# Seven of the eight slices of the second chunk's mixing, issued inside the first down output instead of as a block ahead of it

## The chip, the core and the metric

The kernel runs on one core of one Trainium2 chip. The metric is the device time of one execution in microseconds (us), lower is better; three executions were taken, and the median counts. A core has TensorE (PE, with its weight loads as PEld), VectorE (DVE), ScalarE (ACT), GpSimd (POOL) and SyncE (SP), which run their own instruction streams in order and wait for each other through semaphores.

## The reference, cut to what matters

```python
# x (64, 64, 1024), cond (64, 128); K = 8 experts
h   = gelu(cond @ W0 + b0); h = gelu(h @ W1 + b1)
att = softmax(h @ W2 + b2)
agg_w = einsum('bk,koi->boi', att, weight[..., 0])     # a 64 x 64 mixing matrix per batch
agg_b = att @ bias_k
y   = einsum('boi,bih->boh', agg_w, x) + agg_b[:, :, None]
# three ternary linear layers, w -> round(clip(w / (mean|w| + eps), -1, 1)) * mean|w|
out = x + bitlinear(bitlinear(y, w_gate) * bitlinear(y, w_up), w_down)   # 1024 -> 2752 -> 1024
```

## The kernel before

The 4096 rows of x are worked off in 8 chunks of 512 tokens. Per chunk there are three stages on TensorE. The **mixing** (`conv(c, k)`, L698) multiplies x by the block-diagonal matrices of the mixing in KH = 8 slices of 128 columns of H, each slice as four f32 products, which the trace shows as eight records. Slice k goes to one of two PSUM banks, `YB[k % 2]`; from slice 2 on it waits until VectorE has taken slice k - 2 out (`s_yv`, L710). Slice 1 of chunk 1 also waits for the scales of chunk 0 (`s_p2v`) and for transposed tiles that used its bank (L708). Then come the **gate and up** products and last the **down** products.

Chunk 0 is worked in the plain way while the weights come in: 21 full tiles of gate and of up, each followed by transposes of the next quantised weight tiles, in an order that is written out by hand (`order0`, L119 to L153). The last up tile and the last transposes are the last entries of it. ScalarE copies each transposed tile out of PSUM (`copy_T`, L1072; the copies of a tile of w_down are L1092, L1095 and L1098) and counts it on `s_te`, NQ in all. Chunks 1 to 7 use a seven-product scheme in pairs (`product`, L829) and grouped down products (`down_group`, L899); chunk c + 1 is mixed inside these, one slice per pair. Chunk 1 has no such place, so it is mixed as a block between the up tiles and the down outputs of chunk 0 (L977). This is where the change is.

`down(c, d)` (L806) makes one of DN = 8 outputs of 128 tokens x 512 columns of chunk 0: one matmul with the leftover rows (`inter_r`) and two for each of FT = 21 tiles f, 43 in all, in bank `DNB[d % 2]`. Output 0 waits for all weight tiles (`s_te` at NQ, L812) and, tile by tile, for VectorE's low halves (`s_ulo`, L817 and L822). Output d waits for VectorE to have added output d - 2 to xr (`s_o`, L810). `downs` (L943) issues the eight outputs and, when there is a next chunk, behind output 0 the matmul `norms(c + 1)`, which waits for the sum l1 of all eight slices of y (L723), and behind output 1 `norms_T(c + 1)`, four one-column matmuls that wait for p2b (L728), which VectorE makes in `scales`.

On VectorE the order is by hand as well: slice 0 of chunk 1's mixing is taken out (`conv`, L1349, ys at L1360), then the last `split` of chunk 0 (L1571, L1488), then slices 1 to 7. Behind slice k comes the sum of the magnitudes of slice k - 1 (L1375), for which ScalarE makes |y| (`magnitudes`, L1011). Then (L1599 to L1636):

```python
            for j in range(EARLY, first):
                combine(j)
            output(0, 0)
            scales(1)
            for k in range(KH):
                scale_y(1, k)
            sum_quarter(1, S1)
            lo_quarter(1, A11)
            output(0, 1)
```

and so on through output 7, with ten more combinations of weight blocks between the outputs. `combine(17)` to `combine(20)` (L1500; first tensor_tensor at L1509 or L1506) make the weight sums of the seven-product scheme in two staging buffers; ScalarE fills part of them (`copies`), GpSimd stores them to DRAM (L648), and a buffer is used again when its store has landed. `scales(c)` (L1377) reads the norms matmul and writes p2b at L1389. SyncE stores output d when `s_o` has counted it, loads the first ring blocks of the combined weights behind output 5 (L584 to L588), and the first combined down weights behind the last output (L593).

Of the kernel before, what the change touches and what calls it, by code (L numbers as in the profile page):

```python
# [5 lines left out]
def adaln_ternary_ffn(nc: bass.Bass, x, cond, w0, b0, w1, b1, w2, b2, wk, bias_k, w_gate, w_up, w_down, out):  # L6
# [18 lines left out]
    KH = H // P  # L25
# [49 lines left out]
    def hidden(n):  # L75

        return n if n < NG else (n - 1) % NG

    summed = [e for e, (n, s, _, _) in enumerate(loads) if s]
    q_load = {n: e for e, (n, _, q, _) in enumerate(loads) if q}  # L80
    assert len(summed) == NQ and sorted(q_load) == list(range(NQ))

# [74 lines left out]
    with ctx:  # L157
# [64 lines left out]
        def raw(e):  # L222
            n, _, _, s = loads[e]
            return slot(*s)[0:tiles[n][1], 0:tiles[n][2]]

        def part(f, i):

            return inter[:, f, :].bitcast(f16)[:, i * TOK:(i + 1) * TOK]
# [426 lines left out]
        def _(pe):  # L655
            def mm(o, l, r, start=True, stop=True):
                return nc.tensor.matmul(o, l, r, start=start, stop=stop)  # L657
# [40 lines left out]
            def conv(c, k):  # L698

                if k == 0:  # L700
                    pe.wait_ge(s_x, 16 * (c + 1))
                    pe.wait_ge(s_ablk, 2 * (c + 1))
                if k == 0 and isinstance(c, int) and c == 0:
                    pe.wait_ge(s_bbv, 1)
                if k == 1 and not (isinstance(c, int) and c == 0):
                    pe.wait_ge(s_p2v, c)
                    if isinstance(c, int) and c == 1:
                        pe.wait_ge(s_te, max(n for n in range(NQ) if n % 3 == 2) + 1)  # L708
                if k >= 2:
                    pe.wait_ge(s_yv, KH * c + k - 1)  # L710
                for t in range(NT):
                    last = mm(YB[k % 2][:, t * P:(t + 1) * P], xa[:, t, k * P:(k + 1) * P], ablk[:, t, :])
                last.then_inc(s_y, 1)
# [56 lines left out]
            def waited(c):  # L770

                if not isinstance(c, int):
                    pe.sem_inc(s_turn_pe, 1)

            def group(c, j):

                if j < 4:
                    if isinstance(c, int) and c == 0:
                        if j:
                            pe.wait_ge(s_agg1, j)  # L780
                    else:
                        pe.wait_ge(s_uv, UP * c)
                elif j - 4 < FT:
                    pe.wait_ge(s_gv, FT * c + j - 3)
                else:
                    pe.wait_ge(s_uv, UP * c + j - 3 - FT)
                waited(c)
                for n, k in enumerate(FIRST_K if j == 0 else range(KH)):
                    if j == 0:
                        pe.wait_ge(s_ylo, KH * c + n + 1)  # L790
                        waited(c)
                    if j < FT:
                        w = wgT[:, k, j * P:(j + 1) * P]
                    elif j == FT:
                        w = wrT[:, k, :]
                    else:
                        w = wuT[:, k, (j - UP) * P:(j - UP + 1) * P]
                    if isinstance(c, int) and c == 0 and j == 0 and n == KH // 2:
                        pe.wait_ge(s_te, 1)
                    if isinstance(c, int) and c == 0 and j == 0 and n == 6:  # L800
                        transpose(1)
                    for i in range(2):
                        last = mm(GUB[j % 4][:, :], w, yp[:, k, i, :], start=(n + i == 0), stop=(n == KH - 1 and i == 1))
                last.then_inc(s_gu, 1)

            def down(c, d):  # L806

                t, n = d // HB, d % HB
                if d >= 2:
                    pe.wait_ge(s_o, DN * c + d - 1)  # L810
                elif isinstance(c, int) and c == 0:
                    pe.wait_ge(s_te, NQ)  # L812
                else:
                    pe.wait_ge(s_o, DN * c)
                cols = slice(n * TOK, (n + 1) * TOK)
                if d == 0:
                    pe.wait_ge(s_ulo, UP * c + 1)  # L817
                waited(c)
                mm(DNB[d % 2][:, :], inter_r[:, t * P:(t + 1) * P], wdT[:, FT, cols], start=True, stop=False)
                for f in range(FT):  # L820
                    if d == 0:
                        pe.wait_ge(s_ulo, UP * c + f + 2)  # L822
                        waited(c)
                    for i in range(2):
                        last = mm(DNB[d % 2][:, :], part(f, i)[:, t * P:(t + 1) * P], wdT[:, f, cols],
                                  start=False, stop=(f == FT - 1 and i == 1))
                last.then_inc(s_dn, 1)
# [115 lines left out]
            def downs(c, more):  # L943
                for d in range(DN):
                    down(c, d)
                    if more and d == 0:
                        norms(c + 1)
                    if more and d == 1:
                        norms_T(c + 1)
# [16 lines left out]
            for what, n in order0:  # L966
# [7 lines left out]
                elif what == "U":  # L974
                    pe.wait_ge(s_te, NG + n + 1)
                    group(0, FT + n)
            for k in range(KH):  # L977
                conv(1, k)
            downs(0, True)

            def pairs(c, more):
# [864 lines left out]
```

## Time and profile before

| | us |
|---|---|
| median of 3 executions (lowest, highest) | 1734.46 (1733.05, 1734.97) |
| the profiled execution | 1734.24 |
| its span, first to last instruction | 1732.4 |
| TensorE busy | 1705.4 (98%) |
| VectorE busy | 1097.0 (63%) |
| ScalarE busy | 576.4 (33%) |
| mean granted TensorE clock (1 is 2.4 GHz) | 0.996 |

The profile is of one execution. Times in the trace are counted from the first instruction of the span. An engine's busy time is what the sum of its instructions covers; matmuls are pipelined, so that the recorded length of a matmul (0.38 us for 512 columns) is longer than the distance to the next one. In a timeline, neighbouring instructions of the same kind are merged into one row.

### The profile page before, as it was taken

What the parts mean: (1) busy time and instruction counts of PE and PEld (TensorE: products, weight loads), DVE (VectorE), ACT (ScalarE), POOL (GpSimd) and SP (SyncE); (2) the same over time, 40 slices, a digit from 0 to 9 for tenths busy, and PEclk for the clock granted to TensorE, in tenths of its full rate; (3) what the DMA queues carried; (4) which work ended last, traced back from release to release, by engine and by line L of the source; (5) the groups of instructions that cost most, each with busy time, mean ns of one, the idle gap of its engine ahead of it and who ended that gap; (6) DMA issues with size and microseconds to landing.
All of it is one profiled execution on the core that took longest, in us unless ns stands there. A gap on an engine that the chain in (4) does not pass through costs nothing.

```text
span 1732.4 us, 31273 instructions
## 1 busy us (share of the span) xinstructions
PE 1705.4 (98%) x12380; PEld 1209.9 (70%) x12388; DVE 1097.0 (63%) x1785; ACT 576.4 (33%) x921; POOL 29.2 (2%) x57
## 2 busy tenths in 40 slices
PE   5999999999999999999999999999999999999999
PEld 3454555977769596795958868597776958678584
DVE  5888896555765458554685546855576555855464
ACT  6777742312333133231333213231233313333120
POOL 0010001000000000000000000000000000000000
PEclk8999999999999999999999999999999999999999
DMA  9656725412232121410224121331223312132021
GB/s 341 248 199 236 252 93 190 148 46 97 75 123 101 41 107 65 180 65 22 107 95 170 65 75 54 121 142 45 97 75 111 112 43 107 65 123 74 31 90 49
DMA packets 59687, 194.06 MB, mean 112 GB/s; under 512 B 5264, under 2 KB 5712, under 8 KB 59536
## 3 DMA queue, kind: packets, MB, share of 16 engines
q1 hardware_dynamic: 56464, 177.62, 28.9%
q0 software_dynamic: 2480, 14.22, 2.2%
q8 instruction: 109, 1.79, 0.4%
q14 instruction: 42, 0.34, 0.1%
q10 hardware_dynamic: 592, 0.09, 0.0%
HBM read 160.90 MB, written 31.01 MB: 111 GB/s over the span
## 4 chain that ended last, share of the span: by engine, by line
PE 96%; SPq 1%; DMA 1%; DVE 1%; ACT 1%; issue 0%; DVEq 0%
PE ps L877 52%; PE ps L934 24%; PE ps L657 16%; PE ps L895 2%; SPq L526 1%; DMA wuT<-in_L_ffn_w_gate_dram 1%; PE ps L757 1%; ACT aT L261 0%; DVE msk L1438 0%; DVE xa L1509 0%; DVE prod L1476 0%; ACT wdT L1092 0%; SPq L490 0%; DVE xa L1512 0%; ACT wgT L1108 0%
## 5 line engine op out<-in xcount | busy, mean ns | idle before, releaser
L877 PE MATMUL ps<-yp,wgT 128*128 128x256 f16 x4116 | 902.6, 273 | 2.4 <-issue 2.2
L877 PE MATMUL ps<-wuT,wgT 128*128 128x256 f16 x4116 | 902.6, 273 | 0.0
L877 PEld LDWEIGHTS ps<-yp,wgT 128*128 128x128 fp8e4 x4116 | 402.9, 98 | 53.1 <-issue 5.3
L877 PEld LDWEIGHTS ps<-wuT,wgT 128*128 128x128 fp8e4 x4116 | 402.7, 98 | 48.3
L934 PE MATMUL ps<-wdT,inter 128*128 128x512 fp8e4 x1960 | 433.2, 379 | 0.0
L934 PEld LDWEIGHTS ps<-wdT,inter 128*128 128x128 f16 x1960 | 191.2, 98 | 227.0 <-issue 1.4
L1743 DVE SCALAR_TENSOR_TENSOR xr<-ps,osc,xr 128x512 f32<-128x512 f32 x210 | 156.6, 749 | 168.0 <-PE ps L934 128.4
L1692 DVE TENSOR_TENSOR wdT<-ps,msk 128x512 f32<-128x512 f32 (+1 forms) x77 | 51.3, 667 | 207.1 <-PE ps L877 207.1
L1221 ACT COPY raw<-ps 128x512 f32<-128x512 f32 (+1 forms) x77 | 43.6, 567 | 316.5 <-PE ps L877 315.9
L1228 ACT COPY msk<-ps 128x512 f32<-128x512 f32 (+1 forms) x77 | 43.6, 567 | 140.5 <-PE ps L877 140.5
L1243 ACT COPY inter<-ps 128x256 f32<-128x256 f32 x70 | 26.1, 372 | 180.1 <-PE ps L877 180.1
L1726 DVE TENSOR_TENSOR inter<-inter 128x1024 f16<-128x1024 f32 x70 | 85.3, 1219 | 0.0
L1185 ACT CAST yp<-ys 128x1024 f16<-128x1024 f32 x49 | 48.5, 1042 | 101.8 <-DVE ys L1393 59.0
L1656 DVE TENSOR_TENSOR wdT<-ps,raw 128x512 f32<-128x512 f32 x70 | 48.4, 692 | 44.8 <-PE ps L877 44.3
L657 PE MATMUL ps<-yp,wgT 128*128 128x512 f16 x336 | 76.1, 379 | 0.1
L657 PE MATMUL ps<-yp,wuT 128*128 128x512 f16 x336 | 75.1, 379 | 0.0
L657 PE MATMUL ps<-wdT,inter 128*128 128x512 fp8e4 x336 | 73.8, 379 | 0.0
L1251 ACT CAST inter<-inter 128x1024 f16<-128x1024 f32 x70 | 73.3, 1047 | 0.0
L1247 ACT CAST inter<-prod 128x768 f16<-128x768 f32 x35 | 29.1, 832 | 132.7 <-DVE prod L1696 132.7
L1678 DVE TENSOR_TENSOR wdT<-ps,raw 128x512 f32<-128x512 f32 (+1 forms) x77 | 50.9, 661 | 33.2 <-ACT raw L1235 33.2
L1247 ACT CAST inter<-wuT 128x768 f16<-128x768 f32 x35 | 29.1, 832 | 127.7 <-DVE wuT L1696 127.7
L657 PE MATMUL ps<-ablk,xa 128*128 128x128 f32 x512 | 69.8, 283 | 1.1 <-DMA xa<-in_x_dram 0.7
(224 smaller groups left out, 1488.6 us busy)
## 6 DMA issues: line engine op xcount, KB each, us to landing
wgT<-wcomb SPq DMA_DIRECT2D x70, 896.0 KB, 4.7
wdT<-dcomb SPq DMA_DIRECT2D x14, 2240.0 KB, 10.4
xa<-in_x_dram SPq DMA_DIRECT2D x8, 2048.0 KB, 7.9
out_dram<-xr SPq DMA_DIRECT2D x64, 256.0 KB, 2.0
wcomb<-xa POOLq DMA_DIRECT2D x17, 448.0 KB, 3.6
xr<-in_L_ffn_w_down_dram SPq DMA_DIRECT2D x9, 512.0 KB, 5.6
inter<-in_L_ffn_w_gate_dram SPq DMA_DIRECT2D x7, 512.0 KB, 16.1
wdT<-in_L_ffn_w_up_dram SPq DMA_DIRECT2D x7, 512.0 KB, 4.2
```

What stands on the lines that cost most here:

```text
L657: return nc.tensor.matmul(o, l, r, start=start, stop=stop)
L877: last = nc.tensor.matmul(out, w, operand(i, OPERAND[what])[:, k, :], start=(start and h + k + i == 0), stop=(k == KQ - 1 and i == 1), ski ...
L934: last = nc.tensor.matmul(bank[:, :], x, wd_block(p, BLOCK[what]), start=(what in ("P1", "P2", "P5") and q + i == 0), stop=(q == GRP - 1 a ...
L1185: nc.scalar.copy(operand(0, s), quarter(s)).then_inc(s_yhi, 1)
L1221: nc.scalar.copy(t1[:, 0:w], PB[p % 2][:, 0:w]).then_inc(s_t1, 1)
L1247: nc.scalar.copy(pair_parts(p, 0, 0, 3), blocks4[p % 2][:, HALF:4 * HALF]).then_inc(s_hiA, 1)
L1251: nc.scalar.copy(pair_parts(p, 0, 3, 4), sums).then_inc(s_hiS, 1)
L1656: V.tensor_tensor(rr if p < NPR else g21, PA[:, 0:w], t1[:, 0:w], ALU.add).then_inc(s_c11, 1)
L1678: V.tensor_tensor(rr[:, TOK - w:TOK], PC[p % 2][:, 0:w], q67[:, 0:w], ALU.add).then_inc(s_c22, 1)
L1692: V.tensor_tensor(rr[:, 0:w], PC[p % 2][:, 0:w], q6[p % 2][:, 0:w], ALU.add).then_inc(s_c12, 1)
L1726: V.tensor_tensor(pair_parts(p, 1, 3, 4), sums, pair_parts(p, 0, 3, 4), ALU.subtract).then_inc(s_loS, 1)
L1743: V.scalar_tensor_tensor(xr[:, t, cols], bank[:, :], osc[:, t:t + 1], xr[:, t, cols], ALU.mult, ALU.add).then_inc(s_o, 1)
```

## The change

In `down`, behind the wait for tile f of output 0, slice f // 3 + 1 of the mixing of chunk 1 is issued if f is a multiple of 3 (f = 0, 3, ..., 18 give slices 1 to 7). The block ahead of the down outputs keeps slice 0 alone. `down` is used for chunk 0 only. Only TensorE's stream is changed; the streams of the other engines are as they were.

```diff
@@ -821,6 +821,8 @@
                     if d == 0:
                         pe.wait_ge(s_ulo, UP * c + f + 2)
                         waited(c)
+                        if f % 3 == 0 and f // 3 in range(KH):
+                            conv(1, f // 3 + 1)
                     for i in range(2):
                         last = mm(DNB[d % 2][:, :], part(f, i)[:, t * P:(t + 1) * P], wdT[:, f, cols],
                                   start=False, stop=(f == FT - 1 and i == 1))
@@ -974,8 +976,7 @@
                 elif what == "U":
                     pe.wait_ge(s_te, NG + n + 1)
                     group(0, FT + n)
-            for k in range(KH):
-                conv(1, k)
+            conv(1, 0)
             downs(0, True)
 
             def pairs(c, more):
```

## Rows read from the trace of the kernel before

**Rows 1.** The page: TensorE's busy time, and the chain that ended last.
```profile
PE 1705.4 (98%) x12380; PEld 1209.9 (70%) x12388; DVE 1097.0 (63%) x1785; ACT 576.4 (33%) x921; POOL 29.2 (2%) x57
...
PE 96%; SPq 1%; DMA 1%; DVE 1%; ACT 1%; issue 0%; DVEq 0%
```

**Rows 2.** Timeline of TensorE: start, length, instruction, count, idle time before and releaser.
```profile
214.07 4.30 PE L657 MATMUL ps<-ablk,xa 128*128 128x128 f32 x32
218.59 4.04 PE L657 MATMUL ps<-ablk,xa 128*128 128x128 f32 x32 [0.22 <-DVE ys L1360]
222.46 0.38 PE L657 MATMUL ps<-wdT,inter_r 128*128 128x512 fp8e4 x1
222.68 9.23 PE L657 MATMUL ps<-wdT,inter 128*128 128x512 fp8e4 x42
231.96 0.38 PE L657 MATMUL ps<-wdT,inter_r 128*128 128x512 fp8e4 x1
...
241.34 0.25 PE L657 MATMUL ps<-onesb,l 1*128 1x1 bf16 x4
241.52 0.39 PE L657 MATMUL ps<-wdT,inter_r 128*128 128x512 fp8e4 x1
```

**Rows 3.** Timeline of TensorE in chunk 0's mixing: one slice, then the next matmul.
```profile
21.03 1.05 PE L657 MATMUL ps<-ablk,xa 128*128 128x128 f32 x8
21.92 0.38 PE L718 MATMUL ps<-ab,onesb 128*128 128x512 bf16 x1
```

**Rows 4.** Timeline of ScalarE: the last copies of the last transposed tile.
```profile
216.42 0.55 ACT L1098 ACTIVATE wdT<-ps 64x128 fp8e4<-64x128 fp8e4 x2
```

**Rows 5.** Timeline of VectorE beside the mixing and the down outputs.
```profile
215.88 0.68 DVE L1488 TENSOR_TENSOR inter<-prod,inter 128x512 f16<-128x512 f32 x1
...
222.67 0.68 DVE L1360 TENSOR_TENSOR ys<-ps,bbc 128x512 f32<-128x512 f32 x1
...
224.05 0.42 DVE L1375 TENSOR_TENSOR l<-l,ab 128x512 bf16<-128x512 bf16 x1 [0.36 <-ACT ab L1022]
224.40 1.22 DVE L1509 TENSOR_TENSOR msk<-wuT 128x1024 fp8e4<-128x1024 fp8e4 x1
...
230.20 1.23 DVE L1509 TENSOR_TENSOR msk<-wuT 128x1024 fp8e4<-128x1024 fp8e4 x1 [0.55 <-DMA wcomb<-msk]
...
235.48 0.75 DVE L1497 SCALAR_TENSOR_TENSOR xr<-ps,osc,xr 128x512 f32<-128x512 f32 x1
...
237.66 0.41 DVE L1389 CAST l<-p 1x512 bf16<-1x512 f32 x1
...
245.19 0.74 DVE L1497 SCALAR_TENSOR_TENSOR xr<-ps,osc,xr 128x512 f32<-128x512 f32 x1
...
278.85 0.75 DVE L1497 SCALAR_TENSOR_TENSOR xr<-ps,osc,xr 128x512 f32<-128x512 f32 x1 [1.90 <-PE ps L657]
...
288.13 0.75 DVE L1497 SCALAR_TENSOR_TENSOR xr<-ps,osc,xr 128x512 f32<-128x512 f32 x1 [2.22 <-PE ps L657]
```

**Rows 6.** Timeline of TensorE: the two longest stops behind the start.
```profile
36.21 4.49 PE L657 MATMUL ps<-inter 128*64 128x448 f32 x12 [6.68 <-ACT msk L1051]
43.35 0.38 PE L657 MATMUL ps<-tot,ones 128*128 128x1 f32 x2 [2.66 <-DVE tot L1417]
```

**Rows 7.** Windows: stretch, its length, TensorE busy (instructions), granted clock, DMA share, GB/s.
```profile
29.00:30.00 1.00, 0.25 (x4) 1.00 1.02 406
30.00:31.00 1.00, 0.00 (x0) 0.53 1.02 406
40.00:41.00 1.00, 0.69 (x4) 0.85 0.96 197
43.00:44.00 1.00, 0.65 (x3) 0.86 0.10 41
47.00:48.00 1.00, 1.00 (x4) 0.93 0.80 328
```

## The prediction

> **What bounds the kernel now.** I read the page first. TensorE is busy 98% of the span and holds 96% of the chain that ended last [rows 1]: whatever makes TensorE stand still, anywhere, is paid in full, unless it stood still there already. Then the timeline of TensorE over the changed stretch [rows 2]. The reader is to see two blocks there. The mixing of chunk 1 (64 records, eight slices of eight) runs from 214.07 to 222.46, 8.39 us, with one recorded idle time of 0.22. Behind it the down outputs follow each other without a gap: the first from 222.46, the second from 231.96, the third from 241.52. From 222.46 to 231.96 there are 44 matmuls (1 + 42 and the norms matmul), so one costs 0.216 us and an output of 43 costs 9.28.
>
> Is the mixing block at TensorE's own pace? Where a slice stands between other matmuls, the next instruction follows its start by 0.89 us (21.03 to 21.92) [rows 3]. Eight such slices are 7.1 us, so the block holds 1.3 us of waiting: slice k needs the bank of slice k-2, and VectorE takes about 1.0 us per slice (0.68 for ys, 0.42 for l1). That waiting is all that spreading the slices can win on TensorE.
>
> Last I read who is busy beside it. ScalarE still copies the last transposed w_down tile until 216.42 + 0.55 = 216.97 [rows 4], which is under the mixing block. VectorE [rows 5] does the last slice at 222.67, its l1 at 224.05, and then from 224.40, nearly without a gap, the four combinations 17 to 20, output 0 at 235.48, the scales with p2b at 237.66, eight scalings, and so on; it first waits for TensorE at 278.85. TensorE waits for none of this today: p2b is there at 238.07 and is wanted at 241.34, output 0 is there at 236.2 and is wanted at 241.52. The covers are 3.3 and 5.3 us.
>
> **The change part by part.** No instruction is added or dropped; seven slices (56 of the 64 records) move behind f = 0, 3, ..., 18 of output 0. No DMA is moved on any queue, and SyncE and GpSimd keep their order.
>
> (a) Removed: the waiting inside the block. Between two slices now lie six matmuls, 1.3 us, so slice plus matmuls (2.2 us) is longer than VectorE's 1.1. Gain 1.3 us.
>
> (b) The down output needs all tiles (s_te at NQ). Slice 0 ends at about 214.07 + 0.93 = 215.0; the last copy lands at 216.97. Today slices 1 to 7 hide that. Now TensorE waits until about 217.05: 2.0 us lost. Behind this wait on TensorE stand slices 1 to 7 too, and so all of VectorE's work behind them. The wait for s_ulo at f = 20 costs nothing: the last split is done on VectorE right behind slice 0, at 215.88, nine microseconds and more before it is asked for. Nor does the bank of slice 1, whose transposes are long done.
>
> (c) The last slice now ends late. From 217.05: 37 matmuls x 0.216 = 8.0 and 7 slices x 0.89 = 6.2, which is 231.3 against 222.46. VectorE is in order: combinations 17 to 20 stand behind its slice 7. Today ys starts 0.21 behind the end of the slice on TensorE and the first combination 1.73 behind that [rows 5]; so it starts at about 233.2 instead of 224.40, 8.8 us later. VectorE's idle time between the slices is lost.
>
> (d) The norms matmul stands behind output 0 and needs l1 of slice 7. TensorE gets there after six more matmuls, at 232.6; l1 is done at about 233.3: 0.7 us lost. Then 0.22 and 9.28 for output 1: TensorE is at norms_T at 242.8.
>
> (e) norms_T needs p2b. Everything between 224.40 and 238.07 on VectorE is its own work but for 0.55 us on a staging store, which moves along with it (its store is issued by GpSimd behind combination 17). So p2b is there at 238.07 + 8.8 = 246.9: TensorE waits **4.1 us**. Output 2, which also needs output 0 from VectorE (236.2 + 8.8 = 245.0), is covered by that wait.
>
> (f) After that: output 3 needs output 1's accumulation, 245.19 + 0.74 + 8.8 = 254.7, and TensorE wants it at 247.1 + 9.28 = 256.4. It fits by 1.7 us; the later ones fit by more, since their covers were larger. VectorE's delay shrinks by its waits of 1.90 at 278.85 and 2.22 at 288.13 to TensorE's own delay of 5.6. Nothing is late when the products begin. The stores of the combinations and the loads behind them had waits that are longer than the delay, or are released by the down outputs.
>
> Sum: 2.0 + 0.7 + 4.1 - 1.3 = 5.5; directly, norms_T moves from 241.34 to 246.9, 5.6. From there on everything on TensorE lies 5.6 later. The profiled execution took 1734.24 us against a median of 1734.46 and a span of 1732.4, so the sum is made against 1734.24: **1739.8**. Ends of the terms: a slice between f16 matmuls costs 0.89 to 0.97 (its 1/8 of the best stretch in the block, 218.59 to 222.46), up to 0.6 us in all; the semaphore steps 0.2 each way; the staging wait between 0 and 1.1. So 5.0 to 6.6.
>
> (g) The clock. A wait of 4.1 us is not in the sum only by its length. In the trace TensorE stood still for 6.68 us before 36.21 and for 2.66 before 43.35 [rows 6]. The granted clock [rows 7] went to 0.5 (1.2 GHz instead of 2.4) at about 30.0, was back at about 40.3, fell again in the slice 43 to 44 (mean 0.86, so at about 43.7) and rose in 47 to 48 (at about 47.1). So both long stops were followed by the lower level; TensorE then worked 4.1 us and 3.4 us at it, half of which is lost: 2.0 and 1.7 us. Below, the price is nothing, if the clock stays. No row has a stop of 4.1 us, but it lies between these two, and I take the nearer one's 1.7. The stop of 2.0 us in (b) is shorter than either; I count nothing for it, and up to 1.7 in the range.
>
> Of this the Trainium skill speaks in "TensorE: Matmul & The Clock Gate", the section "Why this matters for your kernels": it warns against idle gaps between bursts of matmuls, since such a gap brings TensorE back to the half rate. By that rule the change, which opens a gap in a stretch that has none, costs the 5.6 us and the slow start behind it; without the rule only the 5.6. The trace agrees with it at the two stops above.
>
> Forecast: 1734.24 + 5.6 + 1.7 = **1741.5**.
>
> **The rivals.**
> 1. The same waits, but the clock stays at 2.4 GHz: 1739.8. For it: the last stop before the fall at 30.0 came after sparse work, while here TensorE is dense on both sides. Against: both stops of over 2.5 us fell.
> 2. Both new stops (2.0 and 4.1 us) lower the clock: the first makes slice 7 and so p2b up to 1.7 us later, the second costs 1.7 to 2.0: 1743.3 or so. Against: no stop as short as 2.0 us is seen with a fall.
> 3. VectorE is less late than I count, and p2b is not what TensorE waits for; then (a), (b) and (d) are left: 2.0 + 0.7 - 1.3 = +1.4, 1735.6. It decides if VectorE's chain from 224.40 to 238.07 could be shortened by over 4 us. Against: it shows 0.55 us of idle time.
> 4. The other side: not slower. The place is L1360, for which the block waits; spreading removes 1.3 us, and if the copies of the last tile came before 215.0 and VectorE's work had room, 1734.24 - 1.3 = 1732.9 would stand, a difference under what can be told. The turning points are 216.97 against 215.0, and 3.3 us of cover for p2b against 8.8 of delay. The rows speak against both.
> 5. The change does not do what it says: if the slices were issued as before, nothing would move. The code leaves no room for that: f // 3 runs over 0 to 6, so slices 1 to 7 are all issued in output 0, once each. I give it no chance.
>
> **How the numbers follow.** Forecast 0.50, rival 1 0.26, rival 2 0.14, rival 3 0.07, rival 4 0.03. A measurement of this kernel tells about 0.2% from no change, 3.5 us: between 1731.0 and 1737.9 is "same". The forecast and rivals 1 and 2 are slower by more: 0.89 with a little taken off for a sum that is short by 2 us. Rivals 3 and 4 are within it: 0.10. Faster by over 0.2%: 0.01, since at most 1.3 us can be won. The range: rival 1 with the lower end of the terms is 1734.2 + 5.0 = 1739.2, less 0.7 for the spread of the runs: 1738.5. Rival 2 with the upper ends, 1734.2 + 6.6 + 1.7 + 1.7 = 1744.2: 1744.0. Left out are rivals 3 and 4 and the tails, some 0.15.
>
> **What would show it.** In the trace of the changed kernel: TensorE idle about 2.0 us behind slice 0, released by the ScalarE copy of L1098; about 0.7 before the norms matmul; about 4.1 before the four one-column matmuls of norms_T, released by L1389 on VectorE, at about 247; combination 17 at about 233 instead of 224.40; a granted clock under 1 for three to four microseconds behind 247. The outputs 2 to 7 then without a gap, and the first product some 5.6 to 7.3 us later than today. It is wrong if VectorE starts combination 17 well before 232, if norms_T follows output 1 without a wait, or if a second large wait appears in outputs 3 to 7 (then VectorE, not p2b alone, has become the bound, and the time is above the range).

## The result, and the profile after

The changed kernel takes 1743.9 us (median of 4, 1742.66 to 1745.44) against 1734.01 us (median of 4) for the kernel before; the ratio is 1.0055, with a 95% interval of 1.0042 to 1.0067. It is slower by 9.9 us in the medians. The profiled execution took 1742.93 us with a span of 1741.1, 8.7 more than the span before.

The timeline of TensorE in the changed kernel (start, length, instruction, count, idle time before and its releaser) answers to [rows 2]:

```profile
213.96 1.16 PE L657 MATMUL ps<-ablk,xa 128*128 128x128 f32 x8
216.90 0.39 PE L657 MATMUL ps<-wdT,inter_r 128*128 128x512 fp8e4 x1 [1.79 <-ACT wdT L1099]
217.13 1.05 PE L657 MATMUL ps<-ablk,xa 128*128 128x128 f32 x8
218.02 1.46 PE L657 MATMUL ps<-wdT,inter 128*128 128x512 fp8e4 x6
...
230.24 1.05 PE L657 MATMUL ps<-ablk,xa 128*128 128x128 f32 x8
231.13 1.46 PE L657 MATMUL ps<-wdT,inter 128*128 128x512 fp8e4 x6
233.43 0.38 PE L657 MATMUL ps<-wdT,inter_r 128*128 128x512 fp8e4 x1 [0.84 <-DVE l L1376]
233.65 9.23 PE L657 MATMUL ps<-wdT,inter 128*128 128x512 fp8e4 x42
246.78 0.26 PE L657 MATMUL ps<-onesb,l 1*128 1x1 bf16 x4 [3.90 <-DVE l L1390]
246.97 0.61 PE L657 MATMUL ps<-wdT,inter_r 128*128 128x512 fp8e4 x1
247.37 11.65 PE L657 MATMUL ps<-wdT,inter 128*128 128x512 fp8e4 x42
258.86 0.38 PE L657 MATMUL ps<-wdT,inter_r 128*128 128x512 fp8e4 x1
```

Three stops are new: 1.79 us for the last transposed tile, 0.84 ahead of the norms matmul for l1, 3.90 ahead of norms_T for p2b. Between two slices there is no stop any more: a slice (0.89) and six matmuls (1.29) follow each other every 2.18 us. The three stops are 6.53 us, while norms_T moves from 27.27 to 32.82 us behind slice 0 (241.34 - 214.07 and 246.78 - 213.96), so about 1.0 us of waiting inside the block was won. And output 2 takes 11.89 us (246.97 to 258.86) where output 1 takes 9.3.

VectorE's timeline, which answers to [rows 5], shows why p2b is late. It idles 1.2 us before nearly every slice, then does after 233.06 what it did before the change after 224.40:

```profile
229.15 0.69 DVE L1361 TENSOR_TENSOR ys<-ps,bbc 128x512 f32<-128x512 f32 x1 [1.16 <-PE ps L657]
...
231.33 0.69 DVE L1361 TENSOR_TENSOR ys<-ps,bbc 128x512 f32<-128x512 f32 x1 [1.16 <-PE ps L657]
...
233.06 1.22 DVE L1510 TENSOR_TENSOR msk<-wuT 128x1024 fp8e4<-128x1024 fp8e4 x1
...
238.87 1.23 DVE L1510 TENSOR_TENSOR msk<-wuT 128x1024 fp8e4<-128x1024 fp8e4 x1 [0.55 <-DMA wcomb<-msk]
...
246.31 0.41 DVE L1390 CAST l<-p 1x512 bf16<-1x512 f32 x1
```

The windows of TensorE behind the long stop (stretch, its length, busy, granted clock, DMA share, GB/s) show the other part:

```profile
244.00:246.00 2.00, 0.00 (x0) 0.86 0.26 101
246.00:248.00 2.00, 1.22 (x7) 0.50 0.69 264
248.00:250.00 2.00, 2.00 (x7) 0.50 0.00 0
250.00:252.00 2.00, 2.00 (x6) 0.50 0.00 0
252.00:254.00 2.00, 2.00 (x10) 0.93 0.00 0
```

The clock falls at about 245.4, inside the stop (the first window's mean is 0.86), and is back at about 252.3. That is 6.8 us at the lower level; 1.3 of them lie inside the stop, and TensorE works the other 5.5 us at 1.2 GHz.

To keep the parts apart, each kernel below is read in three stretches of its profile: to the start of slice 0 of chunk 1; from there to the first product of chunk 1 (**the down stretch**, where the change is); and from that product to the end of the span (**the loop stretch**). The first is not touched by the edits down to run 8, and still varies between their profiles (213.5 to 215.9 us). Before the change the others are 297.21 - 214.07 = 83.14 and 1732.4 - 297.21 = 1435.19. In the changed kernel the first product is at 305.26, so they are 91.30 and 1435.84: +8.16 and +0.65.

### The profile page after: what moved, and what is told of

Read it like the earlier page. It is cut to its first block, busy times and chain, and to the rows that moved or that the text cites. A ratio compares the mean times of both kernels' runs of the same rounds, so it can differ in the third digit from the quotient of the medians.

```text
span 1741.1 us, 31279 instructions
## 1 busy us (share of the span) xinstructions
PE 1707.2 (98%) x12380; PEld 1210.3 (70%) x12388; DVE 1096.8 (63%) x1785; ACT 576.6 (33%) x921; POOL 29.5 (2%) x57
## 3 DMA queue, kind: packets, MB, share of 16 engines
q8 instruction: 109, 1.79, 0.4%
## 4 chain that ended last, share of the span: by engine, by line
PE 95%; SPq 1%; DMA 1%; DVE 1%; issue 1%; ACT 0%; DVEq 0%; ACTq 0%; POOLq 0%
PE ps L879 52%; PE ps L936 24%; PE ps L657 16%; PE ps L897 2%; SPq L526 1%; DMA wuT<-in_L_ffn_w_gate_dram 1%; PE ps L757 1%; DMA wcomb<-msk 0%; DVE msk L1439 0%; DVE xa L1510 0%; DVE prod L1477 0%; ACT wdT L1093 0%; SPq L490 0%; DVE xa L1513 0%; DVE msk L1510 0%
```

## The experiments

All medians stand beside those of the kernel before on the same chip: 1734.72 us for the first four kernels, 1734.28 for the next four, 1733.96 for the three with early matmuls, 1733.49 for the last. Runs 1 to 5 start from the changed kernel, runs 7 and 9 to 11 from the kernel before.

**1. Filling the long stop.** To hold the clock without touching the wait:

```diff
                     if more and d == 1:
+                        for _ in range(16):
+                            mm(ps[0][:, :], part(0, 0)[:, 0:P], wdT[:, 0, 0:TOK])
                         norms_T(c + 1)
```

> The changed kernel with 16 more matmuls of 512 columns between output 1 and norms_T; their result (bank 0) is not used. They take 16 x 0.216 = 3.5 us out of the 3.9 us in which TensorE waits for p2b, so TensorE is idle for 0.4 us and never stops. Theory (the wait costs its length, 5.6 us in all, and on top the lower clock behind it, 2.6 us in the profiled run): norms_T at the same place, about 246.8; the granted clock stays at 1; output 2 takes 9.3 us and not 11.9; 1734.0 + 5.6 = 1739.6 against 1743.9. Rival (output 2 is slow because VectorE or a transfer disturbs it, or the extra comes from elsewhere): 1743 to 1744, output 2 still about 11.9.

Measured: 1750.42 us, ratio 1.0084 (1.0069 to 1.01). That is neither of the two. The trace has to be read by stretches. TensorE around norms_T:

```profile
235.12 12.68 PE L657 MATMUL ps<-wdT,inter 128*128 128x512 fp8e4 x58
248.27 0.25 PE L657 MATMUL ps<-onesb,l 1*128 1x1 bf16 x4 [0.47 <-DVE l L1392]
248.45 0.39 PE L657 MATMUL ps<-wdT,inter_r 128*128 128x512 fp8e4 x1
...
257.74 0.38 PE L657 MATMUL ps<-wdT,inter_r 128*128 128x512 fp8e4 x1
```

Slice 0 starts at 215.43 here, so norms_T comes 32.84 us behind it, as in the changed kernel (246.78 - 213.96 = 32.82): the wait is where it was, TensorE only does something in it. The clock stays at 1, and output 2 takes 9.29 us instead of 11.89. The down stretch is 88.71, 5.57 over the kernel before. So the theory holds where the change is: 5.6 us for the waits, 2.6 for the clock. But the loop stretch, which the edit does not touch, is 1444.86, 9.7 us longer. Runs 9 to 11 take that up.

**2. The slices closer together.** At f = 0 to 6 instead of 0, 3, ..., 18:

```diff
-                        if f % 3 == 0 and f // 3 in range(KH):
-                            conv(1, f // 3 + 1)
+                        if f + 1 in range(1, KH):
+                            conv(1, f + 1)
```

> The changed kernel with slices 1 to 7 at f = 0 to 6 instead of f = 0, 3, ..., 18: the same number of slices in output 0, only closer. Theory (how late the last slice is decides, because VectorE's work stands behind it): last slice ends at 217.05 + 0.2 + 6 x 1.33 + 0.9 = 226.1, 3.7 later than before the change, p2b at 241.8; TensorE is there at 241.3 + 2.0 - 1.3 = 242.0. No wait at norms_T, no fall of the clock; what is left is 2.0 for the last transposed tile less 1.3 of waiting in the block: 1734.0 + 0.7 = 1734.7. Rival (interleaving as such costs, by switches between the two kinds of matmul or by VectorE and TensorE disturbing each other): 1738 or more.

Measured: 1736.26 us, 1.0009 (1.0 to 1.0018). The down stretch is 83.94, 0.80 over the kernel before. norms_T follows without a stop; of the new stops only the one for the last tile is left:

```profile
218.82 0.39 PE L657 MATMUL ps<-wdT,inter_r 128*128 128x512 fp8e4 x1 [1.78 <-ACT wdT L1099]
...
243.94 0.25 PE L657 MATMUL ps<-onesb,l 1*128 1x1 bf16 x4
244.12 0.39 PE L657 MATMUL ps<-wdT,inter_r 128*128 128x512 fp8e4 x1
```

Interleaving as such shows no cost here; spreading the slices over the whole output has one. The median is 1.5 us over that of the kernel before; in the profile, 0.8 us is in the down stretch and 0.9 in the loop stretch (1436.08).

**3 and 4. VectorE's order.** Output 0 and the scales ahead of the four combinations, and then output 1 ahead of the scalings as well (the two edits together):

```diff
+            output(0, 0)
+            scales(1)
             for j in range(EARLY, first):
                 combine(j)
-            output(0, 0)
-            scales(1)
+            output(0, 1)
             for k in range(KH):
                 scale_y(1, k)
             sum_quarter(1, S1)
             lo_quarter(1, A11)
-            output(0, 1)
```

> The changed kernel with output 0 and the scales of chunk 1 moved on VectorE ahead of combinations 17 to 20. p2b is ready at about 236.3, so the 3.9 us at norms_T go, and output 2 starts at 242.9. Theory (VectorE's backlog of 8.7 us is what costs, p2b is only the first place where it shows): output 1 is added at 253.9 to 254.6 as before, while TensorE wants it for output 3 at 252.2, so a new wait of 2.4 us appears there: 2.0 + 0.8 - 1.3 + 2.4 = 3.9, that is 1737.9, and if the clock falls at this wait up to 2 more. Rival (p2b alone is the cost): 2.0 + 0.8 - 1.3 = 1.5, 1735.5.

> As the kernel with the scales first, and output 1 moved on VectorE ahead of the eight scalings. Theory: output 1 is added at about 247.3 and is wanted at 252.2, output 2 at 262.9 and is wanted at about 261.5 to 262, so at most about 1 us of waiting is left at output 4; the sum is 1.5 to 2.5: 1735.5 to 1736.5, clock at 1 throughout. Rival (moving VectorE's work about does not help, since its total is late): 1738 or more.

Measured: 1741.05 us (1.0032, 1.002 to 1.0044) and 1739.5 (1.0026, 1.0016 to 1.0036), more than expected in both. With the scales first, the stop moves to output 3, as the theory says:

```profile
244.90 0.39 PE L657 MATMUL ps<-wdT,inter_r 128*128 128x512 fp8e4 x1
245.13 9.23 PE L657 MATMUL ps<-wdT,inter 128*128 128x512 fp8e4 x42
256.57 0.39 PE L657 MATMUL ps<-wdT,inter_r 128*128 128x512 fp8e4 x1 [2.21 <-DVE xr L1498]
256.80 10.91 PE L657 MATMUL ps<-wdT,inter 128*128 128x512 fp8e4 x42
267.55 0.38 PE L657 MATMUL ps<-wdT,inter_r 128*128 128x512 fp8e4 x1
```

The down stretch is 88.80, +5.66: 1.59 up to output 1 (235.35 less the 215.87 of slice 0 is 19.48, against 17.89), 2.39 at output 3 (256.57 against 244.90 + 9.28), and 1.70 for the clock, since output 3 takes 10.98 us. p2b was only the first place at which VectorE's backlog showed.

With output 1 moved too, the stop at output 3 is gone and one of 1.25 us at output 4 is left. The down stretch is still 87.80, because in this execution the first stop lowered the clock:

```profile
216.40 0.39 PE L657 MATMUL ps<-wdT,inter_r 128*128 128x512 fp8e4 x1 [1.78 <-ACT wdT L1099]
216.63 1.84 PE L657 MATMUL ps<-ablk,xa 128*128 128x128 f32 x8
218.26 2.38 PE L657 MATMUL ps<-wdT,inter 128*128 128x512 fp8e4 x6
220.48 1.05 PE L657 MATMUL ps<-ablk,xa 128*128 128x128 f32 x8
```

One slice and six matmuls take 3.85 us instead of 2.19: 1.7 us for a stop of 1.78. So my sum, with the clock at 1 throughout, missed this; without it the down stretch would be 3.0 us over the kernel before, still more than the 1.5 to 2.5 that I expected. The time itself (1739.5) is what the rival named (1738 or more), and can't tell the two apart. The trace speaks against the rival in so far as the stop at output 3 went when output 1 was moved. Both kernels lose 1.3 us more in the loop stretch (1436.53 and 1436.54).

**5. In between.** Slices at every second tile, f = 0, 2, ..., 12 (`if f % 2 == 0 and f // 2 + 1 in range(1, KH): conv(1, f // 2 + 1)`).

> The changed kernel with slices 1 to 7 at f = 0, 2, ..., 12: between the changed kernel (every third tile) and the one with a slice at every tile. Read from the start of slice 0 to the first product of chunk 1 (83.1 us before, 83.9 with every tile, 91.3 changed), so that neither the start nor the loop behind it matters. Theory: combination 17 starts 5.9 later than before, p2b too, TensorE is 0.7 later, the cover was 3.3: a wait of 1.9 at norms_T, 85.8 us in all if the clock stays at 1, up to 87.5 if this stop lowers it. Rival (what matters is that slices are interleaved, not how late the last one is): as with every tile, 83.9, or as changed, 91.3.

Measured: 1738.85 us (1.0025, 1.0014 to 1.0036), down stretch 87.81, 0.3 above the 87.5 that I gave for the case with the lower clock. The stop at norms_T is 2.12 us, and it too lowered the clock: output 2 takes 10.98 us.

```profile
243.71 0.25 PE L657 MATMUL ps<-onesb,l 1*128 1x1 bf16 x4 [2.12 <-DVE l L1390]
243.89 0.39 PE L657 MATMUL ps<-wdT,inter_r 128*128 128x512 fp8e4 x1
254.87 0.38 PE L657 MATMUL ps<-wdT,inter_r 128*128 128x512 fp8e4 x1
```

Sorted by where the last slice ends, the stop at norms_T is 0, 2.12 and 3.90 us for every tile, every second, every third. That is a cover used up, not a cost of interleaving.

**6. Three slices ahead.** Slices 0 to 2 stay a block, slices 3 to 7 go to f = 0 to 4:

```diff
-                        if f % 3 == 0 and f // 3 in range(KH):
-                            conv(1, f // 3 + 1)
+                        if f + 3 in range(3, KH):
+                            conv(1, f + 3)
...
-            conv(1, 0)
+            for k in range(3):
+                conv(1, k)
             downs(0, True)
```

> Slices 0 to 2 as a block ahead of the down outputs, slices 3 to 7 at f = 0 to 4. The block covers the copy of the last transposed tile (to 216.97), and the last slice ends at about 223.4, 1.0 later than before, under the cover of 3.3. Theory: neither of the two costs is left and the 1.2 us of waiting in the block is won: 81.9 to 82.2 us from slice 0 to the first product against 83.1, time 1732.9 to 1733.4 and, with what the loop behind adds in builds with more instructions ahead of it (0.6 to 1.3), no change that can be told. Rival (the last tile still holds output 0 up, or VectorE does not keep up with the closer slices): 83 or more.

Measured: 1734.7 us (1.0004, 0.9995 to 1.0012), down stretch 82.36, 0.78 less than before. No stop of TensorE is left in it:

```profile
214.70 3.10 PE L657 MATMUL ps<-ablk,xa 128*128 128x128 f32 x24
217.64 0.39 PE L657 MATMUL ps<-wdT,inter_r 128*128 128x512 fp8e4 x1
217.94 1.13 PE L657 MATMUL ps<-ablk,xa 128*128 128x128 f32 x8
```

The gain is a little under the 0.9 to 1.2 I expected, and the loop stretch (1435.64) gives half of it back. By its time the version can't be told from the kernel before.

**7. The wait alone.** In the kernel before, `conv(1, 0)`, then `pe.wait_ge(s_te, NQ)`, then slices 1 to 7 as a block.

> The kernel before with only the wait for all weight tiles put behind slice 0; the slices stay a block. It is the first cost by itself, and it delays VectorE too, but by less than the cover. Theory: TensorE waits 1.8 us; the block behind it runs at the same pace or a little faster, so its end is 1.4 to 1.8 later; no wait at norms_T: 84.5 to 84.9 us from slice 0 to the first product, and 0.8 more in an execution in which the clock falls at this stop. Rival (any delay of VectorE comes through in full): 86 or more.

Measured: 1735.79 us (1.0009, 1.0 to 1.0018), down stretch 84.52, +1.38, and no stop at norms_T. The last slice ends 1.38 us later, and so does VectorE's work behind it, but that costs nothing more, being under its cover:

```profile
216.86 6.98 PE L657 MATMUL ps<-ablk,xa 128*128 128x128 f32 x56 [1.78 <-ACT wdT L1100]
223.68 0.38 PE L657 MATMUL ps<-wdT,inter_r 128*128 128x512 fp8e4 x1
```

**8. The changed kernel again.**

> The changed kernel once more, for the clock. Theory: the length of the wait at norms_T is the same in every execution (3.9 us), what varies is how long the lower clock lasts behind it and whether the stop of 1.8 us in front lowers it too (in the kernel with output 1 moved it did, in three others it did not). So norms_T comes 32.8 us behind slice 0, or 33.6 where the first stop lowers the clock, and the median lies above the 1742.9 of the profiled execution: 1743.5 to 1744.5. Rival (the 9.9 us of the comparison are a steady cost of which the profile shows only 8.7): the same local figures as in the first profile, all runs within 1 us.

Measured: 1743.78 us, 1.0052 (1.0039 to 1.0065), as expected. One of the six executions took 4404.84 us, for which nothing on record gives a cause; the others lie between 1742.27 and 1744.63. In the second profile norms_T comes 247.44 - 214.60 = 32.84 us behind slice 0, behind a stop of 3.92. The first stop did not lower the clock here either. The lower clock begins at about 246.6 and lasts to about 253.5, again 6.8 us, of which only 0.8 lie inside the stop, and output 2 takes 12.16 us:

```profile
247.44 0.26 PE L657 MATMUL ps<-onesb,l 1*128 1x1 bf16 x4 [3.92 <-DVE l L1390]
247.63 0.61 PE L657 MATMUL ps<-wdT,inter_r 128*128 128x512 fp8e4 x1
259.79 0.38 PE L657 MATMUL ps<-wdT,inter_r 128*128 128x512 fp8e4 x1
```

```profile
246.00:248.00 2.00, 0.56 (x5) 0.66 0.85 334
252.00:254.00 2.00, 2.00 (x8) 0.63 0.00 0
```

So the length of the stop is steady, and what is lost to the clock behind it is not: 2.6 and 2.9 us in two executions. The down stretch is 91.59, and the span of this profile (1742.3) is 9.9 us longer than that of the kernel before, as much as the medians differ. How often the first stop lowers the clock in this kernel stays open; two profiles are too few.

**9 to 11. The loop stretch.** The kernel before, with n more small matmuls in the stop of 6.68 us near the start [rows 6]:

```diff
             norms_T(0)
+            pe.wait_ge(s_yv, KH)
+            for _ in range(n):
+                mm(ps[6][:, 256:384], onesb[:, :], onesb[:, :])
             for g in range(OG - 1):
```

> The kernel before with 16 more matmuls of 128 columns (32 TensorE instructions with their weight loads; the result is not used) where TensorE stands still for 6.7 us near the start, so that they cost no time of their own. It asks why the kernel with 16 matmuls more at norms_T lost 9.7 us in the rolled loop of chunks 2 to 6, 200 us later and more, with work that was the same. Theory (the number of instructions ahead of the loop shifts where its code lies, and the jump back to its start then costs more): the stretch from the rest product of chunk 2 to that of chunk 7 takes 1031.5 us as there and not 1021.8, and the stops called issue sum to 8.3 and not 2.2; time 1743.5 to 1744.5. Rival (that loss belonged to the place of the filler or to its bank): 1021.8, 1734.3.

> The same with 8 more matmuls (16 TensorE instructions). Theory of the code's place: another value between 1021.8 and 1031.5 us, neither necessarily half; rival: 1021.8. With a smooth dependence on the number of instructions one would see about 1026.6.

> The same with 32 more matmuls (64 TensorE instructions, 1.8 us of work, still inside the stop of 6.7 us). Theory of the code's place: if the cost goes with the number of added instructions, about 1041; if it goes with the place within some unit of code, anything between 1021.8 and about 1032 again. Rival: 1021.8, 1734.3.

Measured: n = 16 gives 1743.61 us (1.0051, 1.0034 to 1.0068), n = 8 gives 1737.45 (1.002, 1.001 to 1.0029), n = 32 gives 1732.76 (0.9991, 0.9982 to 1.0001). The table gives the distance from the rest product of chunk 2 to that of chunk 7 (`rest`, L882 in the kernel before), with the instructions that the profile counts over those of the kernel before (31273). With n = 32 it is below everything that I had expected (1021.8 to 1041):

| kernel | added | stretch, us |
|---|---|---|
| before | 0 | 1688.32 - 666.52 = 1021.80 |
| changed | 6 | 1696.98 - 674.57 = 1022.41 |
| 8 early matmuls | 16 | 1691.68 - 667.38 = 1024.30 |
| 16 early matmuls | 32 | 1698.54 - 667.45 = 1031.09 |
| changed, long stop filled | 38 | 1704.90 - 673.45 = 1031.45 |
| 32 early matmuls | 64 | 1687.22 - 668.03 = 1019.19 |

Two profiles with the same number of instructions can differ by 0.9 us here: run 7 has none added and takes 1020.87. So the 0.6 us of the changed kernel would not count alone; but all seven profiles with 5 or 6 added (runs 2 to 6 and both of the changed kernel) take 1022.2 to 1023.2. From chunk 1 to chunk 2 the distance is the same, 205.1 us, in the kernel before, in the changed one and in the one with the stop filled. Where the time goes can be seen in the waits of TensorE that have no releaser, in the kernel before, with 16 early matmuls, and with the stop filled (engine, line, us in total, times, longest):

```profile
PE ps L877 <- issue: 2.2, 6, 0.7
```

```profile
PE ps L877 <- issue: 8.3, 7, 2.1
```

```profile
PE ps L879 <- issue: 8.3, 4, 2.2
```

The early matmuls themselves stay in the early stop; slice 0 of chunk 1 starts at 214.9 to 215.6 us in their three profiles, within the spread named above. The waits lie at the return of the rolled loop, where the last product of one chunk is followed by the first of the next: a short stop ahead of that first product, a second some matmuls behind it. With 16 early matmuls, the return from chunk 2 to 3 is:

```profile
707.69 0.38 PE L895 MATMUL ps<-wdT,inter_r 128*128 128x512 fp8e4 x1
707.90 0.59 PE L895 MATMUL ps<-wdT,inter 128*128 128x512 fp8e4 x2
708.65 0.27 PE L877 MATMUL ps<-yp,wgT 128*128 128x256 f16 x1 [0.15 <-issue]
...
711.71 0.27 PE L877 MATMUL ps<-wuT,wgT 128*128 128x256 f16 x1 [2.14 <-issue]
...
712.15 0.42 PE L877 MATMUL ps<-yp,wgT 128*128 128x256 f16 x1
```

Five chunks are in the loop, so it returns four times, and each return has one stop of 1.8 to 2.2 us, which make nearly all of the 8.3. The stops are 6.1 of the 9.3 us by which this stretch is longer. The rest is the clock: behind the stop above, the matmuls of 256 columns follow each other every 0.21 us instead of every 0.11, at a granted clock of 0.50, and the same happens at one more of the four returns (1128.38); in the kernel with the filler it is two of four as well. Each time the lower level lasts 3.4 us.

What is shown: adding TensorE instructions ahead of the loop changes what a return costs, wherever they are added (run 1 put them elsewhere than run 9), and not in proportion; 64 more are better than none. The cause is argued only. The DMA view has transfers of a kind called instruction, and two of them pass near each return that was looked at, one on queue q8 and one on q14: with 16 early matmuls at about 709.4 and 710.4, the second 1.3 us before the long stop ends; with 32 at about 709.7 and 711.0, and there TensorE doesn't stop. A wait for code fits this, but the view does not say which engine's code it is.

**12. Both together.** Three slices ahead, and 32 early matmuls, which alone give a loop stretch of 1432.58 us.

> The version with three slices ahead (82.4 us from slice 0 to the first product, 0.8 less than before) together with the 32 early matmuls (1432.6 us from the first product to the end, 2.6 less than before). If the two are independent: 1734.0 - 0.8 - 2.6 + 1.1 for the later slice 0 that the profiles of the builds with early matmuls show = 1731.7 to 1732.3, faster than the kernel before and than either alone. Its code in front of the loop is 69 instructions longer instead of 64; if those five more shift the loop to a worse place, the stretch behind the first product comes back to 1433 to 1436 and the time to 1732 to 1735.

Measured: 1731.62 us, 0.9988 (0.9979 to 0.9997), just below the 1731.7 to 1732.3 of the theory, and the one version here whose interval lies below 1. Down stretch 82.36 (297.14 - 214.78), loop stretch 1432.96 (1730.1 - 297.14).

## Why the prediction was right, and where its sizes were off

The forecast was 1741.5 us within 1738.5 to 1744.0; 1743.9 is inside, at the edge. The course of events was the one foretold; two sizes were not.

- **(a) and (c).** A slice with its six matmuls takes 2.18 us (I had 2.2), and combination 17 starts at 233.06 (I had 233.2). The waiting that was won is about 1.0 us; I had 1.3. The 0.97 us in the ends of the terms is a quarter of the stretch named there, which holds four slices, not an eighth.
- **(b).** The stop for the last tile is 1.79 us (2.0), released by the ScalarE copy that I named. Run 7 shows it alone: +1.38, less than 1.8, because the block behind it then waits less for VectorE: its recorded stop of 0.22 us is gone, and its end comes 0.40 us sooner behind its start than the stop alone would make it.
- **(d) and (e).** 0.84 (0.7) and 3.90 (4.1). norms_T moved by 5.55 us, against my 5.6. Runs 2, 5 and 7 show the cover: the last slice may be late by the cover of 3.3 us and by as much more as TensorE itself is late at norms_T, and nothing is paid. In run 2 it is 3.6 us late and TensorE 0.8, no stop; in run 5 6.2 and 0.9, which leaves 2.0 for a stop of 2.12; in the changed kernel 8.8 and 1.7, which leaves 3.8 for one of 3.90. Run 3 shows that p2b is not special.
- **(f).** Output 3 came without a wait, and VectorE waited for TensorE again from output 5 on.
- **(g), the term mis-sized.** I took 1.7 us for the clock, from the shorter of two stops in the trace of before. It is 2.6 and 2.9 in two profiles, more than behind the longer stop (2.0). The step that failed is the reasoning "it lies between these two, so its price does". The price is half the time that TensorE works at the lower level after it resumes: 5.5 and 6.1 us here, against 4.1 and 3.4 behind the two stops of the kernel before. How long the lower level lasts does lie between the two: 6.8 us here, against 10.3 behind the stop of 6.68 and 3.4 behind that of 2.66. But of the 10.3 us, 6.2 passed inside the stop, where they cost nothing, and of the 6.8 only 1.3 and 0.8. I carried over the price and not its two parts. Run 1 shows the term alone: it goes to nothing once the stop is filled.
- **(b) again.** I counted nothing for the clock at the first stop. In the two profiles of the changed kernel that was right; run 4 shows that it can cost 1.7.
- **A term left out.** Everything behind the first product was to move unchanged. It grew by 0.65 (0.9 in the second profile), at the returns of the loop. I had also written that no instruction is added; the profile counts 6 more.

So the 1.4 us by which the profiled execution is above the forecast are 0.9 of clock and 0.65 of the loop, less 0.1 for an earlier slice 0; the 2.6 us of the second are 1.2, 0.9 and 0.5 for a later one. Two executions of this kernel differ by up to 2.8 us, so that the median came to lie inside the range by 0.1 is in part luck; the mechanism is not. Rival 2, both stops with the lower clock at 1743.3, came nearest to the number but is not what the profiles show: the clock fell behind one stop only, and cost more there. Rival 1 is out, since the clock fell in both profiles. Rivals 3 and 4 are out by the stop at norms_T; rival 4 named rightly what it would take, and run 6 does just that.

## What to carry to other kernels

Spreading a block of work over the next one saves the waiting inside the block, but it also moves the end of the block; before doing it, list what other engines do in order behind its last piece, and compare the delay with the cover of each of their results. Spread the pieces no wider than it takes to remove the waiting, and leave in front what hides the transfers or copies that the next block needs. When a change puts a stop on a dense TensorE, add the slow restart to its length (1.7 to 2.9 us here, where the clock fell), and when the total doesn't match the stretch that was edited, read the untouched stretches before giving it a cause.

## What was not expected of the hardware

Stops of TensorE of about 2 us in the midst of dense work can lower the clock, and do not always. Those of 2.12 us (run 5) and 2.21 (run 3) did, and so did, in one profile (run 4), the stop of 1.78 us at the last tile. In the seven other profiles with a stop of 1.78 or 1.79 us there (both of the changed kernel, runs 1, 2, 3, 5 and 7) the clock stayed. Of the eight stops of 1.8 to 2.2 us at the loop's returns in runs 1 and 9, four were followed by the lower clock; with 2.21 us it fell once and stayed once. Behind each of these stops with a fall the lower level lasted 3.4 us and cost about 1.7, nearly as much as the stop itself.

The cost of a rolled loop's return on TensorE depends on the code ahead of the loop. With 32 instructions added, five chunks took 9.3 us longer than with none, about 6 in stops and 3 in the lower clock behind two of them; with 64 added they took 2.6 us less, with 16 added 2.5 more. That is nearly as much as the whole change under study, and it is brought on by instructions that stand in a stop far ahead. A difference of 0.1 to 0.5% between two builds of this kernel is therefore no evidence for an edit until the stretches are compared one by one.
